# A transformer layer on one core: the causal mask moves from TensorE to GpSimd, and O leaves PSUM in one copy

## The reference

```python
q = x1n @ Wq_down.T @ Wq_up.T;  c = x1n @ Wkv_down.T     # x1n = layernorm(x)
k, v = c @ k_up, c @ v_up                               # 16 heads of 32
scores = q @ k.T / sqrt(32) - slope[h] * |i - j|        # ALiBi, slope[h] = 0.7071 ** (h + 1)
scores = where(i >= j, scores, -inf)                    # causal
x = x + layernorm(softmax(scores) @ v @ Wo.T)
h = silu(layernorm(x) @ w_gate.T) * (layernorm(x) @ w_up.T)   # 1408 wide, FP4 weights
y = h @ w_down.T
x = x + layernorm(y / rms(y))
```

## Time and profile before

| | |
|---|---|
| median of three runs | 2683.6 us |
| the profiled execution | 2682.99 us, span 2681.0 us |
| mean granted clock of TensorE | 0.975 of full speed |
| PE, ACT, DVE, POOL busy | 94%, 56%, 55%, 17% of the span |

### The profile page before, as it was taken

How to read it: one execution, slowest core, us unless ns; L and a number is a source line. 1 busy time by engine, 2 the same in 40 slices (tenths; PEclk the granted TensorE clock), 3 DMA queues, 4 the chain that set the end, 5 groups by cost and what they waited for, 6 DMA issues and landing times.

```text
span 2681.0 us, 40189 instructions
## 1 busy us (share of the span) xinstructions
PE 2509.6 (94%) x14268; PEld 1171.2 (44%) x14268; DVE 1487.4 (55%) x4194; ACT 1510.5 (56%) x4014; POOL 467.3 (17%) x422
## 2 busy tenths in 40 slices
PE   4569999999999999999999999999999999999978
PEld 3324444444444444444444444444444444444433
DVE  5455556474655647465564745556474655647432
ACT  4484746556474655647465564746556474655610
POOL 0001121121212112121211212121121212112122
PEclk7679999999999999999999999999999999999989
DMA  3202021121202012120201212020120202012000
GB/s 112 52 17 48 17 56 25 48 48 33 63 17 60 21 49 48 33 63 17 61 20 48 48 33 63 17 58 23 49 48 33 64 17 61 19 48 48 17 16 16
DMA packets 99563, 109.75 MB, mean 41 GB/s; under 512 B 22885, under 2 KB 73189, under 8 KB 99301
## 3 DMA queue, kind: packets, MB, share of 16 engines
q1 hardware_dynamic: 99362, 107.19, 14.7%
HBM read 39.24 MB, written 16.78 MB: 21 GB/s over the span
## 4 chain that ended last, share of the span: by engine, by line
PE 77%; ACT 8%; DVE 7%; SPq 3%; issue 2%; POOL 1%; DMA 1%; DVEq 0%; POOLq 0%
PE dense L314 55%; PE psO L508 5%; PE psO L314 3%; PE low L476 3%; PE score L493 3%; ACT arena L685 3%; PE score L476 2%; SPq L1101 2%; DVE st_ln L740 1%; PE score L495 1%; DVE xin L748 1%; ACT low L616 1%; ACT L622 1%; PE low L493 1%; ACT L685 1%
## 5 line engine op out<-in xcount | busy, mean ns | idle before, releaser
L314 PE MATMUL dense<-arena,wgu 128*128 128x512 f16 x4224 | 1002.4, 379 | 11.6 <-DVE tb L842 10.7
L314 PEld LDWEIGHTS dense<-arena,wgu 128*128 128x128 f16 x4224 | 402.7, 97 | 447.1 <-DVE tb L842 18.0
L314 PE MATMUL dense<-wdn,arena 128*128 128x512 f16 x2112 | 536.0, 380 | 2.6 <-POOL arena L1036 2.6
L960 DVE CUSTOM_DVE_ANT_0 low<-low,mmax 128x128 f32<-128x128 f32 (+3 forms) x672 | 279.2, 436 | 290.8 <-PE low L476 287.8
L685 ACT ACTIVATE arena<-score 128x512 f32<-128x512 f32 (+3 forms) x720 | 300.3, 437 | 203.4 <-PE score L495 195.9
L1036 POOL TENSOR_TENSOR arena<-tb,arena 128x512 f16<-128x512 f32 x176 | 203.4, 1155 | 1065.3 <-DVE arena L863 1065.3
L616 ACT ACTIVATE low<-low,ncol 128x128 f32<-128x128 f32 (+3 forms) x672 | 299.8, 446 | 135.6 <-DVE ncol L960 126.4
L616 ACT ACTIVATE score<-score,ncol 128x384 f32<-128x384 f32 x352 | 214.1, 608 | 169.5 <-DVE ncol L960 169.0
L960 DVE CUSTOM_DVE_ANT_0 score<-score,mmax 128x384 f32<-128x384 f32 x352 | 214.8, 648 | 107.8 <-PE score L476 103.0
L314 PEld LDWEIGHTS dense<-wdn,arena 128*128 128x128 f16 x2112 | 186.5, 98 | 166.2 <-issue 8.4
L493 PE MATMUL score<-qst,kst 128*128 128x512 f16 (+3 forms) x784 | 226.0, 306 | 9.4 <-ACT arena L685 8.4
(11 more groups left out here) (140 smaller groups left out, 3099.1 us busy)
## 6 DMA issues: line engine op xcount, KB each, us to landing
qst<-arena SPq DMA_DIRECT2D x384, 64.0 KB, 2.0
kst<-arena SPq DMA_DIRECT2D x192, 128.0 KB, 2.4
xin<-x SPq DMA_DIRECT2D x16, 1024.0 KB, 5.2
x<-x SPq DMA_DIRECT2D x64, 256.0 KB, 2.8
out<-stage SPq DMA_DIRECT2D x64, 256.0 KB, 2.0
qst<-mrow SPq DMA_DIRECT2D x96, 8.0 KB, 1.9
kst<-wo_t SPq DMA_DIRECT2D x1, 1024.0 KB, 9.1
qst<-wq_down SPq DMA_DIRECT2D x1, 768.0 KB, 4.6
```

The costliest lines, as they stand in the source:

```text
L314: ins = nc.tensor.matmul(dst, w, a, start=first and k == 0, stop=last and k == len(tt) - 1)
L960: nc.vector.tensor_tensor_reduce(out=mx_bank(k)[:, 0:wide], in0=mx_bank(k)[:, 0:wide], in1=mmax[:, L - wide:L], scale=-1.0 / S_SCORE, scal ...
```

## The change

1. **Mask.** For heads 2 to 15, `transposed(e)` issues the score matmul alone. ACT then takes the exponential of unmasked scores, and POOL sets the entries with key > query of the tile's first 128 columns to zero, four heads at once, by one `affine_select` (`keep_causal`, 128x4x128 f32) for each block s. Heads 0 and 1 (`STEEP` = 2), whose slopes are the largest, keep the mask matmul too.
2. **P V.** `values(s)` waits for the new semaphore `keep` instead of `exp`, and stands 4 tiles behind (`BEHIND` = 4). At the end of the step the last 12 FFN products go ahead of `values(15)`.
3. **O.** ACT copies psO once in f32 to a new SBUF tile `oc` (`o_copy`); this alone frees the bank (`oh`). DVE makes both f16 parts from `oc` (`o_split`, two instructions in place of one).
4. **y's chain.** `power`, `y_norm` and `y_add` move to 3, 4 and 5 slots behind; `LN1_SLOT` is 44.

```diff
-LN1_SLOT = 45
-BEHIND = 2
+LN1_SLOT = 44
+BEHIND = 4
+STEEP = 2
...
-                        pe.wait_ge(sem["ol"], val("ol", t, 0))
+                        pe.wait_ge(sem["oh"], val("oh", t, 0))
...
-                    nc.tensor.matmul(st_bank(e)[:, 0:wide], kst[:, h, P * kt:P * kt + P],
-                                     qst[:, h, P * kt:L], start=True, stop=False)
-                    nc.tensor.matmul(st_bank(e)[:, 0:P], idbig[:, :], tri_sb[:, :],
-                                     start=False, stop=True).then_inc(sem["st"], 1)
+                    ins = nc.tensor.matmul(st_bank(e)[:, 0:wide], kst[:, h, P * kt:P * kt + P],
+                                     qst[:, h, P * kt:L], start=True, stop=h >= STEEP)
+                    if h < STEEP:
+                        ins = nc.tensor.matmul(st_bank(e)[:, 0:P], idbig[:, :], tri_sb[:, :], start=False, stop=True)
+                    ins.then_inc(sem["st"], 1)
...
-                    pe.wait_ge(sem["exp"], val("exp", t, HG * s + HG))
+                    pe.wait_ge(sem["keep"], val("keep", t, s + 1))
                     if kt == 0 and g > 0:
-                        pe.wait_ge(sem["ol"], val("ol", t, g))
+                        pe.wait_ge(sem["oh"], val("oh", t, g))
...
-                        if e % HG == (HG - 1 + BEHIND) % HG and e >= HG - 1 + BEHIND:
+                        if e % HG == HG - 1 and e >= HG + BEHIND - 1:
                             values((e - BEHIND) // HG)
+                if ffn:
+                    run(cut(NS), ALL_PRODUCTS)
                 values(NG * NT - 1)
-                if ffn:
-                    run(cut(NS), ALL_PRODUCTS)
...
-                def o_high(g):
+                def o_copy(g):
                     act.wait_ge(sem["pv"], val("pv", t, NT * g + NT))
-                    nc.scalar.activation(ot[:, 0, g, :], psO[:, :], ACT.Copy).then_inc(sem["oh"], 1)
+                    if g or not (isinstance(t, int) and t == 0):
+                        act.wait_ge(sem["ol"], val("ol", t, g))
+                    nc.scalar.activation(oc[:, :], psO[:, :], ACT.Copy).then_inc(sem["oh"], 1)
...
-                        if e % (HG * NT) == 1 + BEHIND and e > HG * NT:
-                            o_high(e // (HG * NT) - 1)
+                        if e % (HG * NT) == HG + 1 and e > HG * NT:
+                            o_copy(e // (HG * NT) - 1)
...
-                def o_low(g):
+                def o_split(g):
                     dve.wait_ge(sem["oh"], val("oh", t, g + 1))
-                    nc.vector.scalar_tensor_tensor(ot[:, 1, g, :], psO[:, :], 1.0, ot[:, 0, g, :],
+                    link(t, nc.vector.tensor_scalar(ot[:, 0, g, :], oc[:, :], 1.0, None, ALU.mult))
+                    linked(t)
+                    nc.vector.scalar_tensor_tensor(ot[:, 1, g, :], oc[:, :], 1.0, ot[:, 0, g, :],
                                                    ALU.mult, ALU.subtract).then_inc(sem["ol"], 1)
...
+                def keep_causal(s):
+                    pool.wait_ge(sem["exp"], val("exp", t, HG * s + HG))
+                    diagonal = prob_of(s)[:, :, 0:P]
+                    nc.gpsimd.affine_select(out=diagonal, in_=diagonal, compare_op=ALU.is_ge, fill=0.0, base=0,
+                                            pattern=[[0, HG], [1, P]], channel_multiplier=-1).then_inc(sem["keep"], 1)
...
+                for slot, (low_tiles, exp_tiles) in enumerate(SLOTS):
+                    for e in exp_tiles:
+                        if e % HG == 1 and e > 1:
+                            keep_causal(e // HG - 1)
```

More of the change, by code:

```diff
@@ L171, in layer_program @@
         tri_sb = sb("tri_sb", [P, P], f16)
+        oc = sb("oc", [P, L], f32)
         id32 = sb("id32", [P, P], f32)
@@ L174, in layer_program @@
         idbig = sb("idbig", [P, P], f16)
-        ones = sb("ones", [P, HD], f32)
         ncol = sb("ncol", [P, H * NT], f32)
@@ L217, in layer_program @@
         s_mask = ctx.enter_context(nc.semaphore("s_mask"))
-        s_ones = ctx.enter_context(nc.semaphore("s_ones"))
         s_half = ctx.enter_context(nc.semaphore("s_half"))
@@ L325, in prepare @@
                 pe.wait_ge(s_const, 64)
-                pe.wait_ge(s_ones, 1)
                 pe.wait_ge(s_w, 96)
@@ L538, in step @@
                     for e in exp_tiles:
-                        if e % HG == (HG - 1 + BEHIND) % HG and e >= HG - 1 + BEHIND:
+                        if e % HG == HG - 1 and e >= HG + BEHIND - 1:
                             values((e - BEHIND) // HG)
-                values(NG * NT - 1)
                 if ffn:
                     run(cut(NS), ALL_PRODUCTS)
+                values(NG * NT - 1)
             prepare()
@@ L705, in step @@
                                 y_copy(i)
-                o_high(NG - 1)
                 if ffn:
@@ L710, in step @@
                             y_copy(i)
+                o_copy(NG - 1)
             prepare()
@@ L751, in prepare @@
             def prepare():
-                nc.vector.memset(ones[:, :], 1.0).then_inc(s_ones, 1)
                 nc.vector.memset(half[:, :], -0.5).then_inc(s_half, 1)
@@ L967, in step @@
                     for e in exp_tiles:
-                        if e % (HG * NT) == 1 + BEHIND and e > HG * NT:
-                            o_low(e // (HG * NT) - 1)
+                        if e % (HG * NT) == HG + 1 and e > HG * NT:
+                            o_split(e // (HG * NT) - 1)
                     if ffn:
@@ L978, in step @@
                         for i in range(NT):
-                            if slot == down_done(i) + 3:
+                            if slot == down_done(i) + 4:
                                 y_norm(i)
@@ L992, in step @@
                         normalise("ln1", xin[:, i, :], xin[:, i, :], i).then_inc(sem["ln1"], 1)
-                o_low(NG - 1)
+                o_split(NG - 1)
                 if ffn:
@@ L997, in step @@
                             y_moments(i)
-                        if down_done(i) + 3 >= NS:
+                        if down_done(i) + 4 >= NS:
                             y_norm(i)
@@ L1051, in step @@
                     return
-                for slot in range(NS):
+                for slot, (low_tiles, exp_tiles) in enumerate(SLOTS):
+                    for e in exp_tiles:
+                        if e % HG == 1 and e > 1:
+                            keep_causal(e // HG - 1)
                     if ffn:
@@ L1057, in step @@
                         for i in range(NT):
+                            if slot == down_done(i) + 5:
+                                y_add(i)
                             if slot == down_done(i) + 3:
-                                y_add(i)
-                            if slot == down_done(i) + 2:
                                 power(t, "lo", n_y + i + 1, i, i + 1)
@@ L1063, in step @@
                         power(t, "ln1", n_y)
+                keep_causal(NG * NT - 1)
                 if ffn:
                     for i in range(NT):
-                        if down_done(i) + 2 >= NS:
+                        if down_done(i) + 3 >= NS:
                             power(t, "lo", n_y + i + 1, i, i + 1)
-                        if down_done(i) + 3 >= NS:
+                        if down_done(i) + 5 >= NS:
                             y_add(i)
```

## The result

The changed kernel takes 2606.7 us (median of 4 runs, 2601.55 to 2607.28) against 2684.2 us: ratio 0.9706, 95% interval 0.9689 to 0.9723. The forecast was 2608 us, and 151.4 us for a step.

The account below looks back on a forecast made before the run. TensorE, busy 94%, was taken as the bound, so its removed instructions and waits come off the end: 46.2 + 17.4 + 15.6 - 6 + 2 = 75.2 us, from 2683.0 to 2608 us against the median, range 2595 to 2648 us.

Parts of the forecast that it names:

- Masks: TensorE's list: 56 of 64 mask products an image go, 0.055 us each between starts, 46.2 us in 15 steps.
- the 6 us charged behind the table load: Loss at the logarithm's function tables on ScalarE and for single late selects: 0.4 us a step, bounds 0 to 16 us.
- the sign of being wrong that was set: Wrong if line 508 waits for GpSimd over 1 us a step, line 493 takes up a wait, or select exceeds 2.4 us.
- O's bank: P V of the next group waits for ScalarE's copy alone, so waits of 17.4 and 15.6 us go.
- The select: 16 more GpSimd selects a step at 0.61 us, other end 1.51 us; both fit before P V.
- the 1.95 us of the prediction: Time left behind a group's widest tiles for select and two signals, taken as the tightest place; 0.91 us needed.
- First image: First image, without FFN filling: shorter P V waits and fewer masks gain 2 us, between a loss of 4 and gain of 6.
- The end of the step: Last P V behind 12 products that cover its exponential and select; ScalarE's y copy first, VectorE's split before y's statistics: 0.
- GpSimd becomes the bound: Rival, 0.05: selects of 3.0 us give 2734 us; decides from 2.7 us a select, costs nothing below 2.4 us.
- the waits only move: Rival, 0.15: P V waits for the select as long as before for O, only the masks pay, 2637 us.
- more than forecast: Rival, 0.07: TensorE loses up to 0.2 us more at each wait, and no late-select charge: 2593 us.
- VectorE is held up by GpSimd: Rival, 0.09: selects delay VectorE's SBUF-only instructions, reaching TensorE once or twice a step, 15 to 30 us, some 2630 us.

## Why the prediction was right

- **Masks, 46.2 us less the 6 us charged behind the table load: 40.2.** Measured 39.7 us. The mechanism held; that the two numbers are so close is partly luck. Line 493 took up 4.6 us of the charge, as forecast, and the wait for `kst`, which the forecast did not have, 2.8 us. By its letter this is also the sign of being wrong that was set ("if the exponentials' banks (line 493) take up a wait"): it came true, for 3.9 us against the kernel before. The distance between starts gave the price; the duration would have given four times as much.
- **O's bank, 33 us.** By itself 38.0 us in the median. The steps agree (2.27 us against 2.2); the rest is the first image (2 us), which the forecast had in another term, and 2 us behind step 15. That ScalarE's name on two of the three waits hid VectorE was read rightly from the 0.15 us between the subtraction's end and P V.
- **The sum.** 39.7 + 38.0 = 77.7 us against 77.5 measured. But the parts do not stand alone: with the old distance it is 52 us less, with the old slots of y 97 us, in the old way for O 25 us. O's 5 us above the forecast and the terms of the first image and the step's end below it also cancel in part.
- **The select, nothing a step.** The price of 0.61 us held (0.64 measured), and a whole step of the changed kernel shows no wait of P V for GpSimd. The slack did not hold as worked out. Behind the widest tiles of group 3 there are 2.3 us from the last exponential (1257.92) to P V (1260.22), more than the 1.95 us of the prediction, but that is not the tightest place. The layer norm's `power` was to be done "about when that select's exponentials are". It ends 0.6 us after them (1242.97 against 1242.38), the select behind it is 0.55 us late, and P V follows its end by 0.06 us. That this costs nothing is luck: with 0.7 us more in the block TensorE waits there in every step that has a next image.
- **First image, 2 us gained.** Not seen: step 1 starts at 210.5 against 210.3, so nothing was gained. From 165 to 186 us the granted clock was 0.66 on the mean in the changed kernel (above), so mostly the lower level, and 0.91 in the kernel before:

```profile
165.00:186.00 21.00, 12.23 (x85) 3.75 (x78) 9.65 (x35) 16.80 (x47) 0.00 (x0) 0.91 0.15 51
```

  TensorE had its full clock for less of this stretch, and the new kernels' first images differ by as much (208.2 to 210.7 where nothing waits longer). That the clock ate the gain is argued and not shown, and why it differs was not tried.
- **The end of the step, 0.** The new order costs 0.1 to 0.2 us a step by the step lengths, 0.09 of it shown as the gap between f16 and f32 products.
- **The rival "GpSimd becomes the bound"** was rightly put aside but wrongly sized. Its threshold of 2.7 us (nothing below 2.4) came from GpSimd's load in the last part. The waits begin far below it: at two selects, 1.3 us a block, 17 us were lost, and at three, 2.1 us, 65 us. The term that failed is the load as the measure. The 1.65 us of slack, which the experiments set against it, failed at two selects as well, because it was taken at the wrong place.
- **The rivals "the waits only move" and "more than forecast"**: the first needs the masks alone to pay, and O's new way by itself pays 38 us. The second needs 0.2 us more at each wait from start to start; the steps of that run give 0.07 us more for all three.
- **The rival "VectorE is held up by GpSimd"**: seen (0.84 us for line 752 on `stage`, selects of up to 1.12 us), and a whole step shows no wait of TensorE that comes of it. The Trainium skill has the rule (SBUF — State Buffer, Who interferes with whom) that VectorE in a two-port mode and GpSimd block each other for a whole instruction at their shared ports; the trace agrees so far as both sides have longer durations here.

## What to carry to other kernels

Work moved to an idle engine is free only if its result is due later than its queue lets it come: price it by the slack at its tightest place and by what stands ahead of it in that queue, not by the engine's busy share. Here 15 of the 16 selects of the step shown had time to spare, and the one behind the layer norm's `power` had none. With the same `power` one slot later and y's chain earlier, the kernel took 97 us more. And look for the tightest place along the whole queue: doubling the new instruction found it in one run, where reading the widest tiles had not. Where a PSUM bank is read by two engines, let one copy free it; and where a wait is named after an engine long done, look for the semaphore that arrived last.

## What the runs showed of the hardware

- After a stop of TensorE of 3.9 us the granted clock was 0.50 (from 1287.8 to 1291.2 us in the kernel with the old slots of y), in all 14 steps looked at. After a stop of 2.1 to 2.5 us (kernel before with P V 4 tiles behind) it fell in 4 of 14 steps, and such a step is 1.6 us longer. The stops at P V of the kernel before, three a step and 1.5 us at most, left it at 1.00.
- Where the f32 products of 32 columns follow 12 f16 products, TensorE takes 0.09 us longer to come to them than to f32 transposes.
- A 128x4x128 f32 select on GpSimd takes 0.64 us, hardly more than the 128x512 bf16 select of the kernel before (0.61 us), and half of the two-operand addition of line 1042 (1.27 us).
